# Local transformer of a gated four-layer block: mask added by VectorE, maxima subtracted by GpSimd, three sequences under way, PSUM banks by function, weights loaded in parts

## The reference

```
x = attn_layer(shift_tokens(x), Wqkv[i], q_scale[i], k_scale[i], Wo[i]) + x
x = ffn_layer(shift_tokens(x), ln_g[i], ln_b[i], W1[i], b1[i], W2[i], b2[i]) + x
```

## Time and profile before

| | |
|---|---|
| median of 3 runs | 2872.39 us |
| time of the profiled execution | 2870.65 us |
| its span, first to last instruction | 2868.8 us |
| TensorE busy | 2667.4 us, 93% |
| VectorE busy | 1976.4 us, 69% |
| ScalarE busy | 1771.4 us, 62% |
| GpSimd busy | 1305.5 us, 46% |
| mean granted TensorE clock | 0.979 |

### The profile page before, as it was taken

The page is one execution under the profiler, slowest core; times in us unless marked ns, Lnnn a source line. Parts: engine busy times, 40 slices in busy tenths (PEclk is TensorE's granted clock), DMA queues, the critical chain, the costliest instruction groups (busy, mean ns, idle before and its releaser), DMA issues.

```text
span 2868.8 us, 103417 instructions
## 1 busy us (share of the span) xinstructions
PE 2667.4 (93%) x41474; PEld 1961.0 (68%) x41474; DVE 1976.4 (69%) x4817; ACT 1771.4 (62%) x3791; POOL 1305.5 (46%) x1725
## 2 busy tenths in 40 slices
PE   7689999999999999999999999999889988899898
PEld 5556666666666666666666666666677877799767
DVE  6767776777767776777777777777656777555565
ACT  5567666776767766776776766767644336433365
POOL 5554554455454554455455454554433116300373
PEclk9999999999999999999999999999999989999999
DMA  2100001000010001000010000000000200000022
GB/s 81 66 13 15 11 15 52 16 14 12 16 52 15 11 15 52 16 14 12 16 52 15 15 11 17 15 11 15 12 5 4 79 1 7 3 1 0 3 71 83
DMA packets 51095, 66.71 MB, mean 23 GB/s; under 512 B 24521, under 2 KB 30356, under 8 KB 49428
## 3 DMA queue, kind: packets, MB, share of 16 engines
q1 hardware_dynamic: 50964, 64.87, 8.1%
HBM read 38.23 MB, written 1.05 MB: 14 GB/s over the span
## 4 chain that ended last, share of the span: by engine, by line
PE 51%; DVE 21%; POOL 13%; issue 9%; ACT 5%; POOLq 1%; DVEq 1%; SPq 0%; DMA 0%; ACTq 0%
PE ps L853 6%; POOL area L1574 6%; PE ps L814 5%; DVE area L2069 4%; POOL area L1568 4%; DVE area L2037 4%; PE ps L775 4%; DVE area L2039 4%; PE ps L781 4%; PE ps L956 3%; PE ps L940 3%; PE ps L941 3%; PE ps L880 2%; PE ps L846 2%; DVE ssq L2023 2%
## 5 line engine op out<-in xcount | busy, mean ns | idle before, releaser
L1132 ACT ACTIVATE area<-ps 64x128 f32<-64x128 f32 (+4 forms) x1520 | 769.8, 532 | 446.5 <-PE ps L781 131.0
L1568 POOL TENSOR_TENSOR area<-area 128x512 f32<-128x512 f32 x384 | 489.0, 1274 | 817.8 <-DVE area L2039 817.8
L1574 POOL TENSOR_TENSOR area<-area,rnq 128x512 f32<-128x512 f32 x384 | 396.9, 1044 | 14.4 <-ACT rnq L1266 0.6
L775 PE MATMUL ps<-lw,area 128*128 128x512 f32 x768 | 399.6, 623 | 0.7 <-ACT area L1132 0.7
L2023 DVE TENSOR_REDUCE ssq<-area 128x8 f32<-128x512 f32 x384 | 261.3, 681 | 35.9 <-ACT area L1248 24.5
L2095 DVE SCALAR_TENSOR_TENSOR area<-ps,lcol,area 128x128 f32<-128x128 f32 (+1 forms) x288 | 82.9, 343 | 276.2 <-ACT area L1289 272.2
L781 PE MATMUL ps<-ident,area 128*128 128x128 f32 x1536 | 241.8, 280 | 33.5 <-POOL area L1574 32.0
L2039 DVE TENSOR_TENSOR area<-ps,table 128x512 f32<-128x512 f32 x384 | 261.0, 680 | 0.0
L2037 DVE TENSOR_TENSOR area<-ps,table 128x512 f32<-128x512 f32 x384 | 259.6, 676 | 0.4 <-issue 0.4
L1248 ACT ACTIVATE area<-ps 128x512 f32<-128x512 f32 x384 | 227.3, 592 | 43.6 <-PE ps L775 43.6
L781 PEld LDWEIGHTS ps<-ident,area 128*128 128x128 f32 x1536 | 171.4, 144 | 75.2 <-POOL area L1574 73.6
(11 more groups left out here) (304 smaller groups left out, 5744.7 us busy)
## 6 DMA issues: line engine op xcount, KB each, us to landing
lvm<-area SPq DMA_DIRECT2D x384, 65.0 KB, 2.0
lw<-in_wqkv SPq DMA_DIRECT2D x6, 1536.0 KB
area<-in_moe_w SPq DMA_DIRECT2D x24, 256.0 KB, 2.7
lw<-in_wout SPq DMA_DIRECT2D x6, 512.0 KB
ctxT<-in_ctxT SPq DMA_DIRECT2D x64, 38.5 KB, 1.8
lw<-in_moe_w SPq DMA_DIRECT2D x8, 256.0 KB, 2.8
lw<-in_wff SPq DMA_DIRECT2D x6, 341.0 KB
lw<-in_moe_g SPq DMA_DIRECT2D x1, 1152.0 KB
```

The costliest lines, as they stand in the source:

```text
L775: nc.tensor.matmul(ps[s][:, j, :], xsT[s], wqkv[w.p][:, j * 512:(j + 1) * 512], start=True, stop=True).then_inc(l_qk_ps, 1)
L1132: return nc.scalar.activation(dst, src, ACT.Identity if kw else ACT.Copy, **kw)
L1568: pool.tensor_tensor(QR[s][:, cols], QR[s][:, cols], RA[s][:, cols], ALU.add).then_inc(l_rsum, 1)
L1574: pool.tensor_tensor(rows, rows, rnq[s][:, 8 * j:8 * j + 8, None].to_broadcast([S, 8, LD]), ALU.mult).then_inc(l_qkn, 1)
```

## The change

1. `scores` no longer writes the mask: L806 and the bf16 tensors go, the 64 products start their banks themselves. VectorE adds the mask (`masked`, PSUM plus `band_f`) into LP in SBUF, and takes the maxima there. The subtraction of the maxima, in place in LP, is GpSimd's.
2. `halves(a, b)` becomes `stages(a, b, c)`: each sequence passes through three calls, so three are under way; a and c share a buffer set. All orders on the four engines are new, and ScalarE's c takes over the tail of b's softmax. `hidden`, `down` and `gelu` are called for each chunk apart.
3. PSUM is one tensor of 8 banks, and each function has its bank whatever the sequence.
4. The weights come as 15 DMAs in 12 parts (Wqkv in six of 256 KB, Wout in two), one part behind each of the sequences 2 to 13 of a layer, for the layer after it. SyncE's program is unrolled over the 16 sequences there. The first loads ahead of the local transformer are cut in the same way.

```diff
+        banks = ctx.enter_context(nc.psum_tensor("ps", [128, 8, 512], F32))
+        ps = [banks[:, 4 * s:4 * s + 4, :] for s in range(G)]
+        lb_tokens, lb_qk, lb_qkT, lb_v = 3, (4, 3, 4, 0), (3, 0, 2, 5), (1, 5)
+        lb_scores, lb_probs, lb_pv = ((1, 2), (1, 2)), (5, 4), ((2, 3), (2, 3))
+        lb_outputs = (7, 4)
+        lb_project, lb_shift, lb_xnT, lb_up, lb_down = 7, 7, 0, (6, 7), 6
...
                 with engine.Fori(0, IT - 1) as pr:
-                    halves((1, At(p, lp, pr)), (0, At(p, lp, pr)))
-                    halves((0, At(p, lp, pr + 1)), (1, At(p, lp, pr)))
+                    stages((0, At(p, lp, pr + 1)), (1, At(p, lp, pr)), (0, At(p, lp, pr)))
+                    stages((1, At(p, lp, pr + 1)), (0, At(p, lp, pr + 1)), (1, At(p, lp, pr)))
...
+            def layer_and_next_weights(l, p):
+                parts = layer_parts(p, l + 1)
+                for n in range(B):
+                    middle_values(n % G, l * B + n)
+                    if n == 2:
+                        sp.wait_ge(ffn_done, G + l * B)
+                    if 2 <= n < 2 + len(parts):
+                        for dst, src in parts[n - 2]:
+                            sp.dma_start(dst, src).then_inc(lw_loaded[p], 16)
...
+            def masked(s, w, m):
+                V.tensor_tensor(LP[s][:, m * 512:(m + 1) * 512].rearrange("p (c k n) -> p k c n", k=2, n=64), near_scores(m),
+                                band_f[:, None, None, :].to_broadcast([S, 2, 4, 64]), ALU.add).then_inc(l_masked, 1)
...
+            def differences(s, w, m):
+                P = heads8(LP[s], m)
+                pool.tensor_tensor(P, P, mx[s][:, 8 * m:8 * m + 8, None].to_broadcast([S, 8, 64]), ALU.subtract).then_inc(l_shift, 1)
```

More of the change, by code:

```diff
@@ L518, in _ @@
             behind += [(dst[:, :, :], dram[name], w1_loaded) for dst, name in ((rot, "rot"), (w1, "w1"), (moe1_gu, "moe1_gu"), (moe1_d, "moe1_d"))]
-            behind[8:8] = [(dst, src, lw_loaded[p]) for p in range(2) for dst, src in layer_parts(p, p)]
+            behind[8:8] = [(dst, src, lw_loaded[p]) for p in range(2) for part in layer_parts(p, p) for dst, src in part]
             per = -(-len(behind) // (IT - 1))
@@ L859, in shift_back, with normed_T @@
                 pe.wait_ge(l_y1, nth(0, w.it, s))
[L860 to L861 removed]
+                nc.tensor.matmul(banks[:, lb_shift, 0:64], ident[:, :], y1[s][:, 0:64], start=True, stop=True)
+                nc.tensor.matmul(banks[:, lb_shift, 64:128], shift[:, :], y1[s][:, 64:128],
                                  start=True, stop=True).then_inc(l_sh_ps, 1)
[L864 removed]
+            def normed_T(s, w, near=None):
+                if near:
+                    pe.wait_ge(l_qkT, nth(0, near[1].it, near[0], 4, 2))
                 pe.wait_ge(l_xn, nth(0, w.it, s))
[L866 removed]
+                nc.tensor.transpose(banks[:, lb_xnT, 0:S], xn[s][:, :], ident[:, :]).then_inc(l_xnT_ps, 1)
             def up(s, w, value):
[L869 removed]
+                if value == 0:
                     pe.wait_ge(l_xnT, nth(0, w.it, s))
@@ L872, in up @@
                     at = lo if value else HID + lo
-                    last = nc.tensor.matmul(ps[s][0:hi - lo, 1 + value, c * S:(c + 1) * S],
+                    last = nc.tensor.matmul(banks[0:hi - lo, lb_up[value], c * S:(c + 1) * S],
                                             wff1[w.p][:, at:at + hi - lo], xnT[s][:, :], start=True, stop=True)
                 last.then_inc(l_gate_ps, 1)
-            def down(s, w):
-                for c, (lo, hi) in enumerate(HC):
-                    pe.wait_ge(l_hid, nth(0, w.it, s, 3, c))
-                    last = nc.tensor.matmul(ps[s][:, 0, 128:256], hidT[s][0:hi - lo, c, :], wff2[w.p][0:hi - lo, c, :],
-                                            start=(c == 0), stop=(c == 2))
-                last.then_inc(l_ff_ps, 1)
@@ L884, in halves, with down @@
-            def halves(a, b):
-                if a: tokens_T(*a)
+            def down(s, w, c):
+                if c == 0:
+                    pe.wait_ge(l_hid, nth(0, w.it, s, 3, 0))
+                if c == 1:
+                    pe.wait_ge(l_hid, nth(0, w.it, s, 3, 1))
+                if c == 2:
+                    pe.wait_ge(l_hid, nth(0, w.it, s, 3, 2))
+                lo, hi = HC[c]
+                last = nc.tensor.matmul(banks[:, lb_down, 0:D], hidT[s][0:hi - lo, c, :], wff2[w.p][0:hi - lo, c, :],
+                                        start=(c == 0), stop=(c == 2))
+                if c == 2:
+                    last.then_inc(l_ff_ps, 1)
```

560 lines of the change are left out of this document (333 added, 227 removed).

## The result

The changed kernel takes 2675.18 us (median of 4 runs, 2673.42 to 2678.02) against 2871.26 for the kernel before beside it: a ratio of 0.9316, 95% interval 0.93 to 0.9332. It is 31 us faster than the forecast of 2706 and inside the range. Its profiled execution took 2678.02, with a span of 2676.1.

The account below looks back on a forecast made before the run. TensorE was taken as the bound or close to it. 16 (start) + 95 turns x 18.1 + 22 (end) + 8 (tables) + 4 (collisions) = 1769.5 against 1935.2 before, so 2706 us in all; range 2655 to 2800.

Parts of the forecast that it names:

- TensorE's own work: TensorE's work per turn without mask and waits: at most 17.8 us, least 17.5; the sum used 17.8 plus 0.3 of waits.
- the rotation tables: GpSimd's work at each layer's end that still stops it: 5 x 1.6 = 8 us added to the sum.
- The 0.3 us of waits: Waits added to each turn's 17.8 us, the size of the one late link, giving a turn of 18.1.
- the late link: GpSimd's three sums and two normalisations end at 16.0, where TensorE wants the transposes qkT2(a) at 15.7: 0.3 us late.
- tokens(a) ends at 0.7 to 1.3, wanted at 1.0: VectorE's copy of the tokens for TensorE, possibly held by GpSimd's sums and normalisations; counted as part of the 0.3.
- The walk: Going through the new orders with measured durations: five links have 0 to 0.3 us of slack, one is 0.3 late.
- the two places: VectorE's floor1(a) and tokens(a), within GpSimd's sums and normalisations: each can cost 0 to 1 us, by the rule half an instruction.
- 60 for the mask, 92 for the waits: Split of the forecast 166 us gain: 60 from the mask leaving TensorE, 92 from waits, 14 from stops less replacements.
- nothing in reserve: GpSimd's loop with VectorE takes 17.4 us a turn, beside 17.5 to 17.8 for TensorE's order alone.
- rival A: The GpSimd and VectorE loop becomes the bound: turn 18.9 us, 2782 us in all; chance 0.17.
- Rival C: Slower: VectorE holds GpSimd's instructions in the loop, turn 20.1 us, 2895 us; against it, sums don't grow today; chance 0.08.
- Three stops less collisions: TensorE's stops at layers' ends, 18 us, go with weights in parts; 4 us left for small collisions.

Follow-up runs that it names:

- E1: Changed kernel with VectorE's copy of the tokens issued as a maximum over an axis of length 1 instead of a product with 1.0: 2662.11 us, ratio 0.9261.
- E8: Changed kernel with VectorE's copy of the next tokens moved ahead of the first residual, which then reads Y: 2655.38 us, ratio 0.9242.
- E9: E8 with the norms' floors replaced by a bias in ScalarE's logarithm and the outer loop of layers written out: 2650.61 us, ratio 0.9216.
- E4: Changed kernel with TensorE's four mask products per turn put back, VectorE still adding the mask too: 2771.65 us, ratio 0.9647.
- E7: Kernel before, with only the mask moved to VectorE and the subtraction of the maxima to GpSimd: 2931.96 us against 2872.82, ratio 1.0209.
- E5: Changed kernel with two additions of 128x128 put on GpSimd ahead of the layer norm's deviation in every turn: 2706.43 us, ratio 0.9421.
- E2: Changed kernel with the outer loop over pairs of layers written out on the four compute engines: 2666.8 us, ratio 0.928.
- E3: Changed kernel with the weights loaded whole, in 9 DMAs at once right behind a layer's end: 2691.87 us, ratio 0.9373.
- E6: Changed kernel with the subtraction of the maxima done by VectorE behind each maxima instead of by GpSimd: 2747.48 us, ratio 0.9564.

## Why the prediction was right

**The direction and the bound.** TensorE was the bound with waits in it, and remains it. The prediction said that the turn can fall to TensorE's own work if every link arrives, and it nearly does.

**TensorE's own work: the term of the sum that was mis-sized.** "At most 17.8 us per turn ... I put the least at 17.5", and the sum took the upper figure. It is 17.41 at most, and there is still a wait of 0.11 in that. The waits that I separated in the earlier trace rows were not all: I priced up at the projection's pace, 1.42, and it takes 1.33; that pace was itself too slow (0.118 a pass, and 0.112 now); groups of four transposes that I left at 0.50 and more take as little as 0.43. Taking 17.41 for 17.8 is worth 37 us in the sum and is more than the whole miss of 27 against the profiled execution. The waits and the stop came out 2 us above their terms each, the end 4, what lies around the local transformer 3, and the rotation tables 2 below theirs.

**The 0.3 us of waits: right in size, wrong in place.** Measured: 31 x 0.99 / 95 = 0.32. But the late link was named as the transposes of q and k for GpSimd. That is 4.5 us in ten waits, two at each of five layers' ends. The wait is the held copy of the tokens, which the prediction had in the 0.3 as a part ("tokens(a) ends at 0.7 to 1.3, wanted at 1.0"). It was taken as a mean of something smooth, and is in fact two-valued, 0 or 1 us, by whether the loop's jump back stands ahead of the copy. The walk had the copy's hold, but not the jump. That the mean agrees is luck: 30 of the 31 long turns are set by where the jump falls. E1 and E8 show the hold, E1 the jump's own 0.25.

**The port.** The row told of floors of up to 998 ns, and it is 1225 now. The rule of the Trainium skill that I weighed (SBUF — State Buffer, "Who interferes with whom") made the two places cost half an instruction each. For the tokens the mean is 0.32 a turn, which is a third of the normalisation; the floors, by E9 against E8, cost nothing that shows in the new order, and 25 us in E4. The page's rule that the one which issues first wins fits the copies here: those that started before the normalisation, or level with it, were free, and those behind it were held. The page also says that a reduction never contends on this chip; the trace of E1 agrees, with 274 to 288 ns in 96 copies of the same data, 31 of which started 0.64 to 0.77 after the residual, where the other form was held.

**Mask and subtraction.** 1.04 us on GpSimd was the value taken, 1042 ns is measured; the mask on VectorE 687 and the maxima from SBUF 677, where 680 and 685 were taken. The 60 us are right as a price of TensorE's work, and wrong as a share: in the old order taking them away costs 59 us (E7), in the new order putting them back costs 97 (E4). The split "60 for the mask, 92 for the waits" is not borne out. The mask's part alone makes 1.0209 (E7), the new kernel with the mask's products put back 0.9647 (E4), the whole 0.9308. E4 is not the rest of the change alone: it keeps VectorE's addition of the mask and GpSimd's subtraction. No run has the third sequence with the old way to the exponential, and none separates the third sequence from the banks and the orders, so that what each of these is worth stays open.

**The loop, "nothing in reserve".** It was walked at 17.4. E5 puts it near 17.25 if it bounds there, so rival A was 0.16 us a turn away, and not at zero. Rival C failed as its own sentence against it said: the sums' median is 1278 ns with the six reductions beside them, 1272 in the earlier trace rows before. The hold goes the other way, from GpSimd to VectorE, but for the copies of the last layer.

**Weights and stops.** Taken away were three stops (18 us), 4 left for collisions. Two are gone; one of 6.3 us remains. I had read all three as instructions that arrive late because the weights fill the queues. But the two groups of rows are of two stops, and of two kinds. The earlier trace rows is the one behind the second layer, where the outer loop jumps back, and VectorE's copy stands 3.1 us there too, as it stands 3.4 in the change: this is the stop that is left, and by E2 it has nothing to do with the weights. The earlier trace rows lies in the one behind the first layer, where TensorE alone stands, as it does behind the third. These two are gone, and whole weights don't bring them back (E3); what those delay is the transfers of v. Three stops less collisions were to give 14 us, and 12 were found, by luck. Whether the two that are gone were late instructions or something else, no run here tells apart, as none put parts into the kernel before.

**Rotation tables and ends.** 8 for the tables, 5 x 1.25 = 6.3 found. The start is as forecast, 16.0. The end was 22 and is 26.3: with the third sequence the last one runs through three calls nearly alone, and TensorE waits for ScalarE and VectorE between its steps.

## What to carry to other kernels

Where two engines hold each other up for whole instructions, as here, a small instruction on the critical path costs nothing or most of an instruction of the other engine, by which of the two starts first: take its form or its place out of the hold, rather than count a mean. If every second turn is long, look first at what the code has in every second turn, which here was the loop's jump back of 0.25 us just ahead of that instruction. An operation moved from the bound engine to others need not pay (E7) where the order leaves the bound engine no work for the length of the longer chain; measure the parts singly before dividing a gain between them. And an engine's own work is at most what its groups take in the best turn, not what its mean pace gives.

## What the runs showed of the hardware

The held copy ended 0.09 us after GpSimd's instruction, and a held floor can be nearly as long as a sum (16 elements a partition: 1225 ns at most, beside a sum of 1.28 us that had started 0.09 before it). Copies that started 0.64 us or more after the residual were held by a normalisation that started at 0.53 to 0.56, and copies at 0.55 or less were not; the jump back of the inner loop, which made VectorE's copy 0.2 to 0.3 us later, decided between the two in every second turn of five layers. The jump back of the outer loop, which has two layers in its body, made TensorE stand 3.4 us, with a granted clock of 0.58 from 750 to 755 us, and cost 6.3 us in one trace and 4.3 in another. VectorE's subtraction with both inputs in SBUF took 691 to 703 ns in E6, but in the turn that I looked at it lay where GpSimd was idle, so this says nothing on whether that form is held.
